# A third transformer layer moved into the second layer's block and worked through batch by batch

## What is computed

```
x = x + _L1_ffn_ref(_layernorm(x), ...)          # hidden + gate * aux_out
x = x + _L2_xattn_ref(_layernorm(x), channel_map, conv_w, bn_gamma, bn_beta)
x = x + _L2_ffn_ref(_layernorm(x), W_base, b_base, W_router, lora_A, lora_B)

def _L2_xattn_ref(x, channel_map, ...):          # B, C tokens, L channels
    mask = top k tokens of channel_map, k about 0.6 C      # "crucial"
    crucial, sub = mask * x, (1 - mask) * x
    per batch and channel: max and mean over tokens of both
    A_S1, A_S2 = sigmoid(relu(batchnorm(conv1d(max, mean))))
    return crucial * A_S1 + sub * A_S2
def _L2_ffn_ref(x, ...):
    logits = x @ W_router.T; top 2 of 8 experts, softmax weights w
    h = x @ lora_A;  return x @ W_base.T + b_base + 2 * sum_e w_e h_e @ lora_B
```

## Time and profile before

| | |
|---|---|
| median of 3 runs | 1889.36 us (1887.64 to 1889.57) |
| the profiled execution | 1889.23 us, of it span 1887.5 us |
| mean granted TensorE clock | 0.987 |
| PE, DVE, ACT, POOL busy | 1808.7, 1348.4, 636.3, 614.9 us |

### The profile page before, as it was taken

How to read it: one execution, slowest core, us unless ns; L and a number is a source line. 1 busy time by engine, 2 the same in 40 slices (tenths; PEclk the granted TensorE clock), 3 DMA queues, 4 the chain that set the end, 5 groups by cost and what they waited for, 6 DMA issues and landing times. The chain is left out here.

```text
span 1887.5 us, 29022 instructions
## 1 busy us (share of the span) xinstructions
PE 1808.7 (96%) x10418; PEld 1529.3 (81%) x10418; DVE 1348.4 (71%) x2778; ACT 636.3 (34%) x1749; POOL 614.9 (33%) x366
## 2 busy tenths in 40 slices
PE   7999999999999999998998998879889999999998
PEld 6888889888988888886876664675878888888886
DVE  5666676666666676656547867788778888888886
ACT  3312222222212222224025655530343343334333
POOL 6423332233223322233141003434434333333331
PEclk9999999999999999999999998989999999999999
DMA  5101111111101111110010002010101100111111
GB/s 172 59 7 50 50 52 49 51 49 51 40 9 51 49 51 49 52 57 19 23 45 20 1 26 67 23 62 1 45 23 45 34 33 25 41 33 33 34 34 46
DMA packets 29879, 78.44 MB, mean 42 GB/s; under 512 B 3856, under 2 KB 10704, under 8 KB 29424
## 3 DMA queue, kind: packets, MB, share of 16 engines
q1 hardware_dynamic: 29808, 77.50, 12.3%
HBM read 75.39 MB, written 2.10 MB: 41 GB/s over the span
## 5 line engine op out<-in xcount | busy, mean ns | idle before, releaser
L637 POOL TENSOR_TENSOR l0x_comb<-l0x_neg,l0x_bias 128x1024 f32<-128x1024 f32 x32 | 76.5, 2391 | 428.0 <-DVE l0x_probs L1002 305.2
L900 ACT ACTIVATE l0x_probs_t<-bank 128x512 f32<-128x512 f32 x32 | 19.1, 597 | 541.5 <-PE bank L753 541.5
L2794 POOL TENSOR_TENSOR l3x_q<-l3x_q,l3x_cross 128x512 f32<-128x512 f32 x64 | 89.7, 1407 | 200.1 <-DVE l3x_q L1764 200.1
L38 PE MATMUL bank<-l0x_w_v_hi,ctx_lo 128*128 128x256 f32 x512 | 144.9, 283 | 0.0
L36 PE MATMUL bank<-l0x_w_v_hi,ctx_hi 128*128 128x256 f32 x512 | 144.9, 283 | 0.0
L37 PE MATMUL bank<-l0x_w_v_lo,ctx_hi 128*128 128x256 f32 x512 | 144.9, 283 | 0.0
L886 ACT ACTIVATE l0x_probs<-l0x_probs,l0x_top 128x129 f32<-128x129 f32 x256 | 99.4, 390 | 61.1 <-DVE l0x_top L1006 61.1
L2976 ACT ACTIVATE l3x_probs<-l3x_probs,l3x_top 128x128 f32<-128x128 f32 x256 | 99.1, 389 | 37.4 <-DVE l3x_top L3055 37.3
L629 POOL TENSOR_TENSOR l0x_w_qk_lo<-l0x_raw_qk,l0x_w_qk_hi 128x1024 fp32r<-128x1024 f32 x31 | 75.0, 2420 | 110.6 <-ACT l0x_w_qk_hi L893 110.6
L36 PE MATMUL bank<-l3x_qin_hi,l3x_w_q_hi 128*128 128x512 f32 x256 | 106.0, 414 | 3.1 <-PEq L121 3.1
L36 PE MATMUL bank<-ctx_hi,l0x_w_qk_hi 128*128 128x512 f32 x256 | 100.7, 393 | 8.5 <-DVE ctx_lo L1113 8.5
(11 more groups left out here) (474 smaller groups left out, 5233.7 us busy)
## 6 DMA issues: line engine op xcount, KB each, us to landing
l0x_raw_qk<-L_qk_dram SPq DMA_DIRECT2D x31, 512.0 KB, 5.2
l0x_raw_v<-L_v_dram SPq DMA_DIRECT2D x16, 512.0 KB, 5.6
l0x_raw_o<-L_o_dram SPq DMA_DIRECT2D x16, 512.0 KB, 5.5
l3x_raw<-L_q_dram SPq DMA_DIRECT2D x16, 512.0 KB, 3.5
l3x_raw<-L_o_dram SPq DMA_DIRECT2D x16, 512.0 KB, 3.5
kv_raw<-L_kv_dram SPq DMA_DIRECT2D x8, 512.0 KB, 3.5
l0x_ctx_raw<-ctx_t_dram SPq DMA_DIRECT2D x4, 512.0 KB, 6.4
x<-x_dram SPq DMA_DIRECT2D x8, 256.0 KB, 8.3
```

The lines of the kernel that those rows point to most:

```text
L38: return pe.matmul(out, lhs[1], rhs[0], start=False, stop=stop)
L637: pool.tensor_tensor(comb[:, :, :], neg[:, :, :], bias[:, j:j + 1, :].to_broadcast([P, B, P]), ALU.add).then_inc(comb_ready, 1)
L900: act.activation(probs_t[:, 0:BH, :], bank[6][:, :].rearrange("p (b n) -> p b n", b=BH), ACT.Copy).then_inc(t_act, 1)
L2794: pool.tensor_tensor(dst[:, part], dst[:, part], cross[n][:, :], ALU.add).then_inc(rotated, 1)
```

## The change

The blocks `l2_attention` and `l2_ffn` and the two norm stages ahead of them are gone. A class `L2Layer` (the `mixer`) holds the third layer's work as four queues that are written straight behind the second layer's in the same block. The semaphores are cleared once, ahead of the fourth layer, and no longer between the second and the third.

Both norms of the third layer now go through `Handover`, batch by batch: DVE's statistics and their aggregate (`spread`), three small POOL operations (`root`: L227, L229, L232), one ACT activation (`scale`, L240), four PE transposes (`turn`, L247), one ACT copy (`fill`). The first starts in the loop that still adds to x. DVE masks a batch straight from the PSUM bank (`take_crucial`), three batches behind the additions (LAG). Maxima and means are taken per batch. After the map, ACT scales 24 of the 32 crucial tiles and POOL eight; DVE's `combine` does the rest's scaling and the addition in one operation for each chunk, and the batch is turned back, added, normalised again and given to the logits while the next ones are under way. PE's 34 units are placed anew.

Shortened; unchanged lines of the moved routing and of the map's chain are left out:

```diff
-    ROUTE_BANKS, ATTN_BANKS, TURN_BANKS, AUX_BANKS = (5, 7), (2, 4), (2, 0), (4, 5, 3, 2)
+    ROUTE_BANKS, ATTN_BANKS, TURN_BANKS, AUX_BANKS = (5, 7), (2, 4), (2, 0), (4, 5, 3)
...
-    def look_up(self, pe, half):
+    def look_up(self, pe, half, mixer=None):
         pe.wait_ge(self.t_done, half + 1)
         for b in range(half * BH, (half + 1) * BH):
-            wait(pe, self.aux_read, b - 3)
+            if b == B - 1:
+                mixer.turn(pe, 0)
+            wait(pe, self.aux_read, b - 2)
...
-        self.look_up(pe, 1)
-        self.ahead.multiply(pe, 2)
+        self.look_up(pe, 1, mixer)
...
             dve.wait_ge(self.aux_read, b + 1)
-            core.statistics(dve, b)
+            mixer.norm.spread(dve, b)
+            if b >= mixer.LAG:
+                mixer.take_crucial(dve, b - mixer.LAG)
...
+    def turn(self, pe, b):
+        if b >= self.LAG:
+            pe.wait_ge(self.fc_done, b - self.LAG + 1)
+        self.norm.turn(pe, b)
...
+    def tensor(self, pe):
+        for b in range(1, B):
+            self.turn(pe, b)
+            if b in (2, 4, 5):
+                ahead.multiply(pe, 1)
+        ahead.multiply(pe, 5)
+        pe.wait_ge(self.stat_done, 1)
+        pe.wait_ge(self.means_done, B + self.SUMS)
...
+        mm.then_inc(self.stat_full, 1)
+        ahead.multiply(pe, 3)
+        pe.wait_ge(self.z_done, 1)
...
+        ahead.multiply(pe, 1)
+        pe.wait_ge(self.map_in, 1)
...
+        ahead.multiply(pe, 1)
+        pe.wait_ge(self.map_done, 1)
+        pe.wait_ge(self.loaded, 32)
+        for b in range(B):
+            self.back(pe, b)
+            if b >= 3:
+                self.turn_again(pe, b - 3)
+            if b >= 4:
+                self.logits(pe, b - 4)
...
+        ahead.multiply(pe, 13)
+        pe.wait_ge(self.base_loaded, 32)
...
+        ahead.multiply(pe, 8)
...
+    def sums(self, act, k, b):
+        act.wait_ge((self.fc_done, self.fo_done)[k], b + 1)
+        for c in range(DC):
+            last = act.activation(self.spare[:, b % 2, c, :], ..., accum_out=self.stat[:, c, 2 + k, b:b + 1])
...
+    def scalar(self, act):
+        for b in range(B):
+            self.norm.scale(act, b)
+            if b >= 1:
+                self.fill(act, b - 1)
+            if b in (4, 6):
+                ahead.drain(act, 1)
+            if b in (5, 6):
+                self.sums(act, 0, b - 5)
+        self.fill(act, B - 1)
+        ahead.drain(act, 1)
+        for b in range(2, 5):
+            self.sums(act, 0, b)
+        ahead.drain(act, 1)
+        ahead.high(act, 6)
+        for b in range(5, B):
+            self.sums(act, 0, b)
+            ahead.drain(act, 1)
+        for b in range(self.SUMS):
+            self.sums(act, 1, b)
+            if b == 1:
+                ahead.drain(act, 1)
...
+    def combine(self, dve, b):
+        dve.wait_ge(self.scaled, b + 1)
+        dve.wait_ge(self.scaled_last, b + 1)
+        for c in range(DC):
+            last = dve.scalar_tensor_tensor(self.fc[:, b, c, :], self.fo(b)[:, c, :], self.amap[:, c, 1, b:b + 1],
+                                            self.fc[:, b, c, :], ALU.mult, ALU.add)
...
+        self.combine(dve, 0)
+        for b in range(B):
+            if b + 1 < B:
+                self.combine(dve, b + 1)
+            dve.wait_ge(self.back_full, b + 1)
+            dve.tensor_tensor(x[:, b, :], x[:, b, :], bank[3 + b % 2][:, :], ALU.add).then_inc(self.added, 1)
+            dve.wait_ge(self.added, b + 1)
+            self.norm2.spread(dve, b)
```

More of the change, by code:

```diff
@@ L1215, with l1_and_l2 @@
 L1_GROUPS, L1_QUERIES, L1_DIM = 8, 4, 16
-def l1_layer(core, dram, ahead, ffn):
+def l1_and_l2(core, dram, ahead, ffn, mixer):
     nc, x, bank, psum = core.nc, core.x, core.bank, core.psum
@@ L1252, in l1_layer @@
         ffn.norm.claim()
+        mixer.norm.claim()
+        mixer.norm2.claim()
         made, same_ready, select_ready = sem("made"), sem("same_ready"), sem("select_ready")
@@ L1284, in _ @@
                 sp.wait_ge(pv_full, 2 * B - 2)
-                for i in range(8):
+                for i in range(7):
                     ahead.load(sp, i)
+                mixer.sync(sp)
             @block.gpsimd
@@ L1321, in _ @@
                 ffn.gpsimd(pool)
+                mixer.gpsimd(pool)
             @block.tensor
@@ L1538, in _ @@
                 ffn.scalar(act)
+                mixer.scalar(act)
             @block.vector
@@ L1624, in _ @@
                 add_out(B - 1)
-                ffn.vector(dve)
+                ffn.vector(dve, mixer)
+                mixer.vector(dve)
 KV_GROUPS = 8
@@ L1902, in turn_weights, with tensor @@
         mm.then_inc(self.t_full, 1)
-    def look_up(self, pe, half):
+    def look_up(self, pe, half, mixer=None):
         pe.wait_ge(self.t_done, half + 1)
         for b in range(half * BH, (half + 1) * BH):
-            wait(pe, self.aux_read, b - 3)
-            product(pe, self.core.bank[self.AUX_BANKS[b % 4]][:, :], [self.attn_t[:, b * P:(b + 1) * P]],
+            if b == B - 1:
+                mixer.turn(pe, 0)
+            wait(pe, self.aux_read, b - 2)
+            product(pe, self.core.bank[self.AUX_BANKS[b % 3]][:, :], [self.attn_t[:, b * P:(b + 1) * P]],
                     [self.table[:, :]], True, True).then_inc(self.aux_full, 1)
-    def tensor(self, pe, added, last):
+    def tensor(self, pe, added, last, mixer):
         self.reduce_query(pe, 0)
@@ L2018, in scalar @@
         ahead.high(act, 5)
-        ahead.drain(act, 2)
     def copy_first(self, dve, b):
@@ L2114, in vector @@
             dve.wait_ge(self.y_done, b + 1)
[L2115 removed]
+            dve.scalar_tensor_tensor(x[:, b, :], core.bank[self.AUX_BANKS[b % 3]][:, :], gate[:, b:b + 1],
                                      x[:, b, :], ALU.mult, ALU.add).then_inc(self.aux_read, 1)
             dve.wait_ge(self.aux_read, b + 1)
[L2118 to L2346 removed]
@@ L3145, in build @@
             ffn = L1Ffn(core, dram, later, ahead)
+        with ExitStack() as later:
+            mixer = L2Layer(core, dram, later, ahead, ffn)
         with ExitStack() as early:
@@ L3151, in build @@
             ffn.hold_semaphores()
-            l1_layer(core, dram, ahead, ffn)
+            mixer.hold_semaphores()
+            l1_and_l2(core, dram, ahead, ffn, mixer)
         core.free_semaphores()
@@ L3156, in build @@
                 ahead.hold(kept, ctx_ahead, "_place")
-                l2_attention(core, dram, ahead)
-                ahead.hold_cross(ctx_ahead)
-                l2_ffn(core, dram, ahead)
             l3_layer(core, dram, ahead, out)
```

690 lines of the change are left out of this document (352 added, 338 removed).

## The result

The changed kernel takes 1894.75 us in the median of 7 executions (1892.43 to 1896.7), the kernel before 1889.36 (1887.64 to 1890.22): a ratio of 1.0031, with a 95% interval of 1.0020 to 1.0042. By the medians it is slower by 5.4 us. The range of the prediction holds that, its likeliest case (1892.0, own range 1889.5 to 1894) does not, and "no change that can be told" was the wrong side of the edge of 0.2%. All executions are of the fast kind.

The account below looks back on a forecast made before the run. PE was taken as the bound behind the logits, waiting some 21 us ahead of them for DVE and ACT chains. -4.5 + 2.7 - 11.6 + 15.0 + 1.25 = +2.85 us on 1889.23 gave 1892.0, range 1886.2 to 1895.6.

Parts of the forecast that it names:

- likeliest case: Whole kernel: the forecast of 1892.0 us, +2.85, no change that can be told; own range 1889.5 to 1894, chance 0.42.
- the four stages: Changed stretch cut at conv input, map, logits' end and PE's last unit: -4.5, +2.7, -11.6 and +15.0 us.
- the second stall: Stage 1, DVE's masking 1 waits for turn 1, behind PE's last look-up, which needs addition 4: 2.6 us.
- the first stage: From the second layer's first addition to the conv input `padded`: 4.5 us earlier, with ACT's sums ending at 1210.1.
- the third stage: Map to logits' end: DVE the bound at 2.6 us a batch, 29.2 instead of 40.8, 11.6 shorter.
- the rival of the dear `combine`: DVE's loop behind the map: dearer combines end the logits at 1261.7 to 1263.2, total 1893.9 to 1895.4 us; chance 0.16.
- both of its forms: Loop behind the map: each of 32 `combine` operations takes 0.35 to 0.40 us, or POOL's eight scalings hold them up.
- the block's end: Between PE's last drain and the fourth layer: the semaphore clearing now stands there, 1.25 us longer.
- stage 4: Behind the logits to PE's last unit: 19.7 us of units added, idle and low clock taken off, 15.0 longer.
- the clock stays up: Rival: PE's waits in the front bring no stretch at 0.50; sum -2.6, 1886.6 us; chance 0.16.
- Slower by the clock: Rival: two more 3.4 us stretches at 0.50, between the turns or at the fourth layer's start; 1894.6 us; chance 0.14.
- The break-even: End of the logits: the change neither gains nor loses if they end at 1256.9.

Follow-up runs that it names:

- the low behind the roots: Changed kernel with POOL's filler split low(5) moved from ahead of the third layer's first root to behind its fourth: 1889.72 us, ratio 1.0006 to the kernel before.
- the three edits: Changed kernel with low(5) behind the fourth root, last look-up behind three turns, and three more sets of sums on DVE: 1884.17 us, ratio 0.9972 to the kernel before.

## Why the prediction was right and where it failed

The mechanism was right in the four stages. The first masking was forecast 12.9 behind the first addition and comes 12.5 behind; the second stall, 2.6, is 2.70; the convolution's input 48.2, and it is 47.6; the map 67.5, and 66.4; the logits' end 96.7, and about 94.7; PE's last unit 166.3, and about 164.5. DVE waited 6.71 for ACT's sums at the end of the first stage. Behind the logits PE had no wait over 0.5. One sum inside the third stage does not come out of its own terms: eight batches of 2.6 and a wait of 0.6 are 21.4, and 1232.0 to 1255.0 is 23.0. The loop took 21.2, from 1233.72 to 1254.91, but the tail behind it 5.8 instead of 4.8, so half of the slip was hidden. In the rival of the dear `combine`, 32 operations at 0.35 to 0.40 would add 2.9 to 4.6 over 0.255, not the 1.9 to 3.4 that its logits' ends imply.

`combine` was 0.26 each (1.04 for four, from 1237.83 to 1238.87), as assumed; beside POOL's scalings the first eight took 2.65 instead of some 2.1, so 0.6 and not the 1.6 of the rival, and both of its forms fell. POOL's row there:

```profile
1232.71 4.91 POOL L2239 TENSOR_SCALAR l_fc<-l_fc,l_amap 128x128 f32<-128x128 f32 x8 [4.44 <-DVE l_amap L2518]
```

By the rule of the Trainium skill ("SBUF — State Buffer", on the shared port pair) that was weighed there, such a pair excludes each other for a whole instruction. This trace, whose times on POOL are rough, does not bear that out: POOL's scalings took some 0.66 beside the combines and some 0.62 ahead of them, and the combines 0.33 instead of 0.26, two of them for each scaling. What cost the 0.6 was not tested.

The step that failed is the sum's last, **the block's end**. It had +1.25 for the clearing and nothing for the clock behind it, though the text named PE idling 2 us there as a rival. The wait itself was right (1.5 in the trace). The measured price of the clearing at that place is 3.0 us (0.8 to 5.3), 1.5 of them the fourth layer's start at 0.50 in the trace of every version that has it. With these 1.5 the sum would have been +4.35, 1893.6, over the edge of 0.2%.

A second step failed without showing in the profile at hand: the base. The sum was made against one trace of the kernel before, whose changed stretch had 165.5 us; three more of the old order have 161.0 to 162.2. Above all, stage 4 took 1.7 off for the 3.4 us at 0.50 at 1300.3. The wait of 2.5 ahead of it stands in all four traces, the low clock behind it in one. The changed stretch itself was forecast at 168.3, and is 166.8 and 167.8. So of the 5.4 us by the medians 2.85 were forecast, 1.5 are the clock behind the clearing, and the remaining 1 agrees with a base that is shorter on average than the one trace, by somewhat more than the forecast was too long.

That the four stages came out so near is in part luck, since both sides were measured against that trace. Against the second trace of the kernel before, the conv input comes 2.6 to 3.3 us earlier and not 5.1, and the part from the map to L131 is 6.7 longer and not 4.2.

Of the rivals, "the clock stays up" did not occur: the changed kernel's front has stretches at 0.50 in both traces. "Slower by the clock" is what came, at one of its two places, the fourth layer's start, for 1.5 of its 2.5 us. The break-even of the text was right in kind: with the front 11 us shorter again, the order is faster than before. But it lay too late. It stood at logits that end 93.8 behind the first addition; they end at 94.7 in the changed kernel, which is 5.4 slower, at 89.0 with the low behind the roots, which is level (1.0006), and at 83.5 with the three edits.

What stays open: how often an execution of the kernel before has the low clock at 1177 and 1300, and so where the mean of its stretch lies between 161 and 165.5; four traces do not settle it. And what decides where the low clock falls was not tested.

## What to carry to other kernels

When a stage is spread over engines batch by batch, look on every engine for the bulk operation that stands in the queue ahead of the first small one: here one split of 2.34 us on POOL, and sums on ACT that DVE had time for, cost more than the whole change had lost. Filler that is taken out of a wait comes back at full price where its engine is the bound, wherever there it is put, so count the waits that are left and the units that fit them before moving any. Price a wait of PE together with the clock of what stands behind it, and make the sum against more than one trace of the base, because low-clock stretches shift several microseconds from one part of the program to another. When you fill a wait to keep the clock up, add up the time at the low clock in the whole stretch, not only behind that wait.

## What the runs showed of the hardware

The same code reached the same instruction at 1163.08 in one trace and at 1168.22 in another of the same kernel, with spans of 1887.5 and 1888.5. Beside what both have (at about 863, and some 10 us right ahead of that instruction), one stretch of 3.4 us at 0.50 lies at 1007 in the first, and 6.8 us at 963 and 3.4 us at 1144 in the second. What such stretches cost in one part of the program was for the most part not lost in the next.

A wait of PE that is filled with transposes nobody reads keeps the stretch behind it at 1.00 instead of 0.52. The low clock can come back behind the next wait: with one wait filled the changed kernel had 23.9 us at 0.50 as without. With the waits for mean and variance and two behind the map filled, the three edits went from 17.2 us at 0.50 to 3.5. Whether that gains time depends on who waits for PE there: in the traces 1 to 2 us in the changed kernel and 2.5 with the three edits, and nothing in the kernel before, where 13.8 us at 0.50 became 3.4 and the stretch stayed at 161.
